# Setup of layer 2's adapters: smaller tiles for the gated mix, row groups for the shared adapter, four lo parts on POOL

## What is computed

```python
x = x + _L2_ffn_ref(_L2_cond_ref(x, cond_512, ...), gate, kernel, bias, lora_A, lora_B, lora_A_shared, lora_B_shared)

def _L2_ffn_ref(x, gate, kernel, bias, lora_A, lora_B, lora_A_shared, lora_B_shared):
    B, T, D_IN, D_OUT = (8, 256, 512, 512)
    N_LORAS, RANK = (16, 32)
    base_out = jnp.matmul(x, kernel) + bias
    A_eff = jnp.einsum('bn,nri->bri', gate, lora_A)
    B_eff = jnp.einsum('bn,nor->bor', gate, lora_B)
    Ax = jnp.einsum('bri,bti->btr', A_eff, x_flat)
    delta_flat = jnp.einsum('bor,btr->bto', B_eff, Ax)
    Ax_s = jnp.einsum('ri,bti->btr', lora_A_shared, x_flat)
    delta_flat = delta_flat + jnp.einsum('or,btr->bto', lora_B_shared, Ax_s)
    delta = delta_flat.reshape(x.shape[:-1] + (kernel.shape[-1],))
    return base_out + (SCALING * delta).astype(base_out.dtype)
```

## Time and profile before

| | us |
|---|---|
| median of 3 runs | 1237.67 |
| lowest, highest | 1237.02, 1241.85 |
| span of the profiled execution | 1240.5 |
| PE busy in it | 1192.5 (96%) |
| setup: start to the main block's first matmul | 80.17 |

### The profile page before, as it was taken

One profiled execution on the slowest core, in us unless ns is written; L12 is line 12 of the kernel. 1 busy time (PEld: TensorE's weight loads), 2 busy tenths in 40 slices (PEclk: granted clock), 3 DMA queues, 4 the chain that ended last, 5 costly groups with the idle time before them and its releaser, 6 DMA issues.

```text
span 1240.5 us, 46135 instructions
## 1 busy us (share of the span) xinstructions
PE 1192.5 (96%) x21528; PEld 705.2 (57%) x21528; DVE 519.5 (42%) x1010; ACT 356.9 (29%) x762; POOL 540.5 (44%) x411
## 2 busy tenths in 40 slices
PE   5898999999999999999999999999999999999997
PEld 4345565655565556655555556555565555565565
DVE  6862343443443434343344343444343333434343
ACT  2252243233232223123322222323222222313221
POOL 4656416555334446444155553355354333644400
PEclk9899999999999999999999999999999999999999
DMA  5533100020413000002123000002112000001001
GB/s 149 225 138 137 62 2 2 2 62 22 186 53 121 3 2 2 2 8 90 71 70 138 3 2 2 3 2 96 70 69 80 27 3 2 2 2 54 18 19 52
DMA packets 21454, 63.73 MB, mean 51 GB/s; under 512 B 4528, under 2 KB 5296, under 8 KB 17040
## 3 DMA queue, kind: packets, MB, share of 16 engines
q1 hardware_dynamic: 19488, 60.06, 13.3%
q10 hardware_dynamic: 1776, 0.73, 0.2%
HBM read 42.95 MB, written 17.83 MB: 49 GB/s over the span
## 4 chain that ended last, share of the span: by engine, by line
PE 88%; DVE 3%; issue 2%; DMA 0%; ACT 0%; DVEq 0%
PE bank_b L1311 27%; PE bank_a L117 13%; PE bank_a L104 11%; PE bank_b L104 11%; PE bank_b L87 8%; PE bank_a L1248 5%; PE bank_a L75 3%; PE bank_b L1269 3%; PE bank_b L1263 2%; PE bank_b L1323 2%; PE bank_b L1304 1%; DVE z L1154 1%; PE bank_b L1282 1%; PE bank_b L1292 1%; PE bank_b L1325 1%
## 5 line engine op out<-in xcount | busy, mean ns | idle before, releaser
L920 POOL TENSOR_TENSOR sum_v<-raw_v 128x768 f32<-128x768 f32 x30 | 55.3, 1845 | 581.7 <-ACT raw_v L978 581.7
L1311 PE MATMUL bank_b<-w_hi,y3t_hi 128*128 128x512 f32 x512 | 209.8, 410 | 1.8 <-issue 1.8
L1311 PE MATMUL bank_b<-w_lo,y3t_hi 128*128 128x512 f32 x512 | 203.8, 398 | 4.5 <-issue 4.5
L1311 PE MATMUL bank_b<-w_hi,y3t_lo 128*128 128x512 f32 x512 | 204.5, 399 | 0.0
L117 PE MATMUL bank_a<-y,w_down 64*32 64x512 f32 x3072 | 172.2, 590 | 0.0
L1104 DVE TENSOR_TENSOR x<-bank_b,x 128x512 f32<-128x512 f32 x96 | 66.4, 691 | 203.1 <-PE bank_b L1311 162.8
L972 ACT ACTIVATE y<-bank_a,cb,tab 128x512 f32<-128x512 f32 x64 | 49.6, 777 | 320.8 <-PE bank_a L117 315.7
L104 PE MATMUL bank_a<-y,wv 32*64 32x512 f32 (+2 forms) x3584 | 139.2, 476 | 1.8 <-issue 1.8
L104 PE MATMUL bank_b<-y,wv 32*64 32x512 f32 (+2 forms) x3584 | 138.3, 476 | 0.6 <-issue 0.6
L1311 PEld LDWEIGHTS bank_b<-w_hi,y3t_hi 128*128 128x128 f32 x512 | 97.9, 191 | 35.1 <-issue 13.4
L1311 PEld LDWEIGHTS bank_b<-w_hi,y3t_lo 128*128 128x128 f32 x512 | 97.5, 190 | 27.6 <-issue 4.7
(11 more groups left out here) (193 smaller groups left out, 1497.9 us busy)
## 6 DMA issues: line engine op xcount, KB each, us to landing
w_hi<-w_scratch SPq DMA_DIRECT2D x9, 1024.0 KB, 5.0
w_lo<-w_scratch SPq DMA_DIRECT2D x9, 1024.0 KB, 8.2
x_in<-in_x SPq DMA_DIRECT2D x32, 256.0 KB, 4.3
out_x<-out_tile SPq DMA_DIRECT2D x32, 256.0 KB, 2.4
w_raw<-in_w SPq DMA_DIRECT2D x3, 1024.0 KB, 6.3
w_scratch<-w_hi SPq DMA_DIRECT2D x3, 1024.0 KB, 3.9
w_scratch<-w_lo SPq DMA_DIRECT2D x3, 1024.0 KB, 6.9
w_raw<-w_scratch SPq DMA_DIRECT2D x2, 1024.0 KB, 10.1
```

The costliest lines, as they stand in the source:

```text
L920: ins = g_.tensor_tensor(dst[:, :, at:at + count].rearrange("p r k o -> p r (k o)"), src[:, :, 0:count].rearrange("p r k o -> p r (k o)"), ...
L1311: ins = pe.matmul(lin_ps[b][:], y3t[yi][:, k, P * b:P * (b + 1)], w[use(m) % 2][wi][:, k], start=(k == 0 and i == 0), stop=(k == KB - 1 an ...
```

## The change

Three edits to the setup, and what they need elsewhere.

1. The 512 rows of `a2` and `b2` are put in another order by the host: block `c` of 128 rows holds ranks 8c to 8c+7 of all 16 adapters. `gmat` becomes one 128 x 64 matrix (8 batch rows x 8 ranks), made by one POOL instruction instead of four, and each block needs one matmul of 128 x 64 that writes 64 rows of a bank: 4 matmuls for `b2` and 4 for `a2` in place of 8 and 8. The DRAM scratch is indexed to match.
2. The shared adapter is loaded four times, once into each group of 32 partitions, so that the four matmuls of L690 use four row groups. ACT issues 8 DMAs for it where it issued 2.
3. ACT makes the five small hi parts right after evacuating convolution 2 (before the `b2` hi part) and no longer after the down weights. POOL makes four of the five small lo parts, after it has scaled the second group's input and before `blurred(1)`. DVE keeps `b3` alone.

```diff
-    as2 = sb("as2_raw", [R2, LEN])
-    bs2 = sb("bs2_raw", [R2, LEN])
+    as2 = sb("as2_raw", [P, LEN])
+    bs2 = sb("bs2_raw", [P, LEN])
...
-    gmat = sb("gmat", [P, 4, 8, R2])
+    gmat = sb("gmat", [P, 8, 8])
...
-                ("as2", as2[:], io["as2"]), ("bs2", bs2[:], io["bs2"]),
+                *(("as2", as2[R2 * p:R2 * (p + 1)], io["as2"]) for p in range(KB)),
+                *(("bs2", bs2[R2 * p:R2 * (p + 1)], io["bs2"]) for p in range(KB)),
...
             evacuate_2(0)
             evacuate_2(1)
+            for name, raw, hi, *_ in small:
+                act.wait_ge(loaded[name], 16 * (len(PASSES) if name == "b3" else 1))
+                a.activation(hi, raw, ACT.Copy).then_inc(small_hi, 1)
...
             ins.then_inc(down_ready, 1)
-            for name, raw, hi, *_ in small:
-                act.wait_ge(loaded[name], 16 * (len(PASSES) if name == "b3" else 1))
-                a.activation(hi, raw, ACT.Copy).then_inc(small_hi, 1)
...
-            for kk in range(4):
-                g.tensor_tensor(gmat[:, kk], gate_t[:, kk].unsqueeze(2).broadcast_to((P, 8, R2)),
-                                delta[:].unsqueeze(1).broadcast_to((P, 8, R2)), ALU.mult).then_inc(gm_ready, 1)
+            g.tensor_tensor(gmat[:], gate_t[:].unsqueeze(2).broadcast_to((P, 8, 8)),
+                            delta[:].unsqueeze(1).broadcast_to((P, 8, 8)), ALU.mult).then_inc(gm_ready, 1)
...
             scaled_input(1)
+            for k, (*_, raw, hi, lo) in enumerate(small[:-1]):
+                pool.wait_ge(small_hi, k + 1)
+                g.tensor_tensor(lo, raw, hi.bitcast(F32), ALU.subtract).then_inc(small_lo, 1)
             blurred(1)
...
-            for k, (*_, raw, hi, lo) in enumerate(small):
-                dve.wait_ge(small_hi, k + 1)
-                v.tensor_tensor(lo, raw, hi.bitcast(F32), ALU.subtract).then_inc(small_lo, 1)
+            *_, raw, hi, lo = small[-1]
+            dve.wait_ge(small_hi, len(small))
+            v.tensor_tensor(lo, raw, hi.bitcast(F32), ALU.subtract).then_inc(small_lo, 1)
...
-                pe.matmul(w2_ps[p][:], as2[:, p * P:(p + 1) * P], bs2[:], start=True, stop=True).then_inc(w2_done, 1)
-
-            pe.wait_ge(gm_ready, 4)
+                rows = slice(R2 * p, R2 * (p + 1))
+                pe.matmul(w2_ps[p][:], as2[rows, p * P:(p + 1) * P], bs2[rows], start=True, stop=True).then_inc(w2_done, 1)
+
+            pe.wait_ge(gm_ready, 1)
...
-                    for kk in range(4):
-                        last = pe.matmul(banks[h][:], g2[:, kk, h * P:(h + 1) * P], raw[:, kk],
-                                         start=(kk == 0), stop=(kk == 3))
+                    for c in range(2):
+                        last = pe.matmul(banks[h][P // 2 * c:P // 2 * (c + 1)], g2, raw[:, 2 * h + c], start=True, stop=True)
...
-            "a2": nc.dram_tensor("a2_scratch", [2, 8, R2, LEN], F32).ap(),
+            "a2": nc.dram_tensor("a2_scratch", [2, 4, 8, R2 // 4, LEN], F32).ap(),
```

More of the change, by code:

```diff
@@ L179, in setup_program @@
     b3 = sb("b3_raw", [len(PASSES) * E3 * R3, LEN])
-    as2 = sb("as2_raw", [R2, LEN])
-    bs2 = sb("bs2_raw", [R2, LEN])
+    as2 = sb("as2_raw", [P, LEN])
+    bs2 = sb("bs2_raw", [P, LEN])
     w2, w0_add = (sb(n, [P, KB, LEN]) for n in ("w2", "w0_add"))
-    gate_t = sb("gate_t", [P, 4, 8])
-    delta = sb("delta", [P, R2])
-    gmat = sb("gmat", [P, 4, 8, R2])
+    gate_t = sb("gate_t", [P, 8])
+    delta = sb("delta", [P, 8])
+    gmat = sb("gmat", [P, 8, 8])
     a2eff = [keep["w_sum"][:, 2 * i:2 * i + 2].bitcast(F32R) for i in range(2)]
@@ L266, in _ @@
                 for h in range(2):
-                    sp.dma_start(scratch[name][i, 4 * h:4 * h + 4].rearrange("b r n -> (b r) n"),
+                    sp.dma_start(scratch[name][i, 2 * h:2 * h + 2].rearrange("c b j n -> (c b j) n"),
                                  eff[i][:, h].bitcast(F32)).then_inc(out[2 * i + h], 16)
@@ L683, in _ @@
             conv2_tiles(pe, bank_a, keep, 1).then_inc(keep["c2_done"], 1)
-            pe.wait_ge(loaded["as2"], 16)
-            pe.wait_ge(loaded["bs2"], 16)
+            pe.wait_ge(loaded["as2"], 16 * KB)
+            pe.wait_ge(loaded["bs2"], 16 * KB)
             pe.wait_ge(keep["y2_ends"], 1)
             for p in range(KB):
-                pe.matmul(w2_ps[p][:], as2[:, p * P:(p + 1) * P], bs2[:], start=True, stop=True).then_inc(w2_done, 1)
-            pe.wait_ge(gm_ready, 4)
+                rows = slice(R2 * p, R2 * (p + 1))
+                pe.matmul(w2_ps[p][:], as2[rows, p * P:(p + 1) * P], bs2[rows], start=True, stop=True).then_inc(w2_done, 1)
+            pe.wait_ge(gm_ready, 1)
             pe.wait_ge(loaded["a2"], 16)
             pe.wait_ge(loaded["b2"], 16)
-            g2 = gmat[:].rearrange("p k b r -> p k (b r)")
+            g2 = gmat[:].rearrange("p b j -> p (b j)")
             for banks, raw, done, added in ((b2_ps, b2, b2_done, 2), (a2_ps, a2, a2_done, KB)):
@@ L834, in load_adapters @@
                         sp.dma_start(keep["a2s"][rows, g].bitcast(F32),
-                                     scratch["a2"][i_a][2 * it + g]).then_inc(adapters_loaded, 16)
+                                     scratch["a2"][i_a][:, 2 * it + g]).then_inc(adapters_loaded, 16)
                         sp.dma_start(keep["b2s"][rows, g].bitcast(F32),
-                                     scratch["b2"][i_b][2 * it + g]).then_inc(adapters_loaded, 16)
+                                     scratch["b2"][i_b][:, 2 * it + g]).then_inc(adapters_loaded, 16)
             def load_raw(l):
@@ L1437, in build @@
             "w2": nc.dram_tensor("w2_scratch", [P, KB, LEN], F32).ap(),
-            "a2": nc.dram_tensor("a2_scratch", [2, 8, R2, LEN], F32).ap(),
-            "b2": nc.dram_tensor("b2_scratch", [2, 8, R2, LEN], F32).ap(),
+            "a2": nc.dram_tensor("a2_scratch", [2, 4, 8, R2 // 4, LEN], F32).ap(),
+            "b2": nc.dram_tensor("b2_scratch", [2, 4, 8, R2 // 4, LEN], F32).ap(),
         }
@@ L1479, in host_layout @@
     b0 = c(i["L0_ffn_Bf"].transpose(0, 2, 1)).reshape(2, P, LEN).transpose(1, 0, 2)
-    a2 = i["L2_ffn_lora_A"].reshape(4, P, LEN).transpose(1, 0, 2)
-    b2 = c(i["L2_ffn_lora_B"].transpose(0, 2, 1)).reshape(4, P, LEN).transpose(1, 0, 2)
+    a2 = i["L2_ffn_lora_A"].reshape(16, 4, 8, LEN).transpose(2, 0, 1, 3).reshape(P, 4, LEN)
+    b2 = i["L2_ffn_lora_B"].transpose(0, 2, 1).reshape(16, 4, 8, LEN).transpose(2, 0, 1, 3).reshape(P, 4, LEN)
     x = i["x"].reshape(GROUPS, ROWS, ROWS, CH, LEN).transpose(0, 1, 3, 2, 4).reshape(GROUPS, P, ROWS, LEN)
@@ L1501, in host_layout @@
         "a2": a2, "b2": b2,
-        "gate_t": np.repeat(i["L2_ffn_gate"].T, R2, axis=0).reshape(4, P, 8).transpose(1, 0, 2),
-        "delta": np.tile(np.eye(R2, dtype=np.float32), (ROWS, 1)),
+        "gate_t": np.tile(i["L2_ffn_gate"].T, (8, 1)),
+        "delta": np.repeat(np.eye(8, dtype=np.float32), 16, axis=0),
         "as2": i["L2_ffn_lora_A_shared"],
```

## The result

The changed kernel takes 1230.62 us (median of 6, 1229.05 to 1235.23) where the kernel before, run beside it, takes 1240.4 (1237.02 to 1242.8): ratio 0.9931, interval 0.9912 to 0.995. I had forecast 2.3 us more, 1240.0 on a median of 1237.67. The profiled execution was the changed kernel's quickest: 1229.05 us, span 1227.2.

What follows compares the result with a forecast made beforehand. PE was taken to bound the kernel, with only the main block's start open. First stretch +4.5, second -3.6, clock +1.4 made +2.3 us: span 1240.5 to 1242.8, median 1240.0 us, range 1232 to 1245.3.

Steps and rivals of the forecast that it cites:

- Six more issues: Setup, ACT: six added DMA issues ahead of the table load delay the square root by 3.5 us (2.7 to 4.4).
- The cover of `gmat`: Setup, POOL and DVE: with one gmat, DVE's table instructions meet POOL's longer additions, 1.0 us more, 0 if let through.
- L690 in row groups: Setup, PE: the shared adapter's matmuls in four row groups take 1.2 us instead of 4.04.
- The mix: Setup, PE: eight 128x64 matmul instructions, two side by side, take 2.0 us instead of 7.13 for sixteen.
- DVE held by POOL: Late setup: each of POOL's three blurred(1) passes holds one DVE table instruction, so DVE ends at 79.0 us.
- Start of the main block: Barrier: SP waits for the b2 lo store's landing at 80.5 us; first matmul at 81.1 against 80.17, +0.9 us.
- The clock behind the barrier: Start of main block: after about 7 us idle, PE gets half its clock, costing 1.4 us (0 to 1.7).
- DVE was held: Rival, late setup: DVE is not held by POOL, the main block starts 4.0 us earlier, 1233.7 us; chance 0.17.
- the issues did reach the path: Rival, ACT in setup: the six issues hide, only 1.0 of 4.5 us stays, 1236.5 us; chance 0.11.
- the tiles ran side by side: Rival, PE in setup: tiles do not run side by side, L690 4.04, each mix 3.6, total 1241.1 us; chance 0.10.
- ACT's queue did not stall: Rival, slower: two more long DMA issues on ACT make the table 8.0 us late, 1245.3 us; chance 0.14.
- both faster rivals together: Setup: DVE is not held by POOL and the six DMA issues hide, 1230.2 us; chance 0.06.

Runs made afterwards that it cites:

- second edit alone: The kernel before with only the shared adapter in four row groups and six more DMAs on ACT; 1245.14 us, ratio 1.0026.
- eight matmuls added: The changed kernel with eight useless matmuls in PE's idle time, giving PE's program its old length from the mix on; 1243.6 us, ratio 1.0012.
- first edit alone: The kernel before with only the 128x64 mix, one gmat and its scratch layout, PE's program 32 instructions shorter; 1230.29 us, ratio 0.9916.
- +256: The kernel before with 64 useless matmuls added in PE's idle time, 256 PE instructions more; 1241.13 us, ratio 0.9998.
- +224: The kernel before with 56 useless matmuls added in PE's idle time, 224 PE instructions more; 1230.74 us, ratio 0.9917.

## Why the prediction was wrong

**The step that failed is the first**: "nearly all of that is the main block, which the change leaves alone. So the question is only when the main block starts". I read the chain of waits, saw PE at 88% and "issue" at 2%, and took those 2%, some 25 us, as given. They are not: they hang on how many instructions stand ahead. The change moves that by 32, which took the pauses of the main block from 18.1 to 9.5 us; with the 32 put back they were 17.1. The waits view from 80 us on would have shown 18 us of pauses with no releaser; no term of my sum, and no rival, had room for it. Only the list of signs named it: "if the main block itself takes another time". The base was low too: the median of three runs that I added 2.3 us to was 1237.67, and the medians of the kernel before taken beside the later runs are 1240.2 to 1241.5.

The other steps, in their order:

- **Six more issues, +3.5 us.** The shared adapter's issues went from two to eight and take 4.6 us; the `eb` issue, 2.19 us before, takes 0.46 now, so the root moved by 1.6 us only. With the same 19 issues it came at 26.92 us in the run with the second edit alone (`cb` took 1.46) and at 27.39 in the run with eight matmuls added (`eb` took 1.99): 3.1 and 3.5 us later than before. Long single issues come in some executions and not in others, with either kernel; so in two traces of three the term was near its size, and the 1.6 is in part luck.
- **The cover of `gmat`, +1.0 us.** The root moved 25.44 - 23.86 = 1.6 us and the table's user 40.03 - 37.27 = 2.8 us, so the additions cost 1.2: right. The first edit alone showed the other side, which I had bounded by 0: there POOL waits for `ob`, and the table comes 4 us earlier, 3.5 of them not from the root.
- **L690 in row groups, 1.2 us:** 1.14, right.
- **The mix, 2.0 us each:** 3.40 and 3.62 us, at half the clock. With the first edit alone, the `a2` mix took 1.94 us at full clock, so the tiles do run side by side; I had not carried PE's idle time inside the setup into the clock.
- **DVE held by POOL, end at 79.0 us:** three holds, end at 78.25. Right in kind and size, on later instructions than I named, since the products were ready later: the mix ran at half the clock, and PE paused 1.67 us within L75.
- **Start of the main block, 81.1 us:** 79.96. The landing of the `b2` store, my last term, did not bind: it came at 78.98 us, before SP's last issue ended at 79.32.
- **The clock behind the barrier, +1.4 us:** 4.89 against 3.40 us, so +1.5, right.

For the setup and the first convolution I had +2.3 and the trace has +1.3. The first edit's mechanism in the setup, that a faster PE ends in a wait for DVE, held. The time came out on the other side by a term that I did not have.

Of the rivals, none happened in this trace: DVE was held, the issues did reach the path, the tiles ran side by side, ACT's queue did not stall (it did in the run with eight matmuls added). That the changed kernel came near the 1230.2 us of both faster rivals together is chance.

## What to carry to other kernels

Where PE bounds the kernel and its chain has "issue" in it, list those pauses before anything else: a change that adds or removes PE instructions anywhere ahead of them moves all of them, and here that was worth 10 us of 1240, more than all three edits did on their own paths. (Three positions out of 256 were timed; the one that the kernel before happened to have was the slow one.) To judge such an edit apart from this, pad PE's program back to the old length modulo 256 instructions and time both. And where an engine's DMA issues stand ahead of a step on the path, issue what is needed late behind that step.

## What the runs showed that I had not expected

- PE's program is read in pieces whose places repeat every 256 instructions: +256 gave the old time (ratio 0.9998), +224 the time of -32 (0.9917 and 0.9916), with pauses at the same instructions.
- The size of a pause can hang on the data traffic beside it: 4.48 us with the data queue at 99.2% of the DMA engines, 1.19 at the same instruction with the stores moved. Six others, of 1.2 to 2.0 us, had no data beside them.
- A pause can cost more than its own length: half the clock followed one of 1.84 us in the kernel before (980.5 to 984 us). It need not: one of 1.91 us in the changed kernel was followed by the full clock.
- The setup does not repeat itself: the same code started the main block at 73.29 and at 77.03 us, where POOL and DVE met 0.3 us apart.
- A short POOL instruction can let DVE through some 3.5 us earlier, if POOL then has to wait for a transfer: the first edit alone, 33.25 us against 37.27, of which 0.5 us is the earlier root.
